# Two rings shared between the sync engine and GpSimd in half tiles every 8 and 12 groups, and the exponentials of layer 0 read from PSUM

## The reference, cut to what matters

```python
edge_index = jnp.stack([src, dst])
h = jnp.maximum(_layernorm(x, axis=-1), 0.0)
x = x + _L0_gnn_ref(edge_index, h, Wq, Wk, Wv, gamma, beta, 8)
h = jnp.maximum(_layernorm(x, axis=-1), 0.0)
x = x + _L1_gnn_ref(h, L1_gnn_beta, edge_index)
...
# layer 0: 8 heads of 16; rows, cols are the two ends of an edge
att = jnp.einsum('ehd,ehd->eh', qE, kE)          # q of one end, k of the other
expAtt = jnp.exp(jnp.clip(att, -10.0, 10.0))
# sums per node of expAtt and of expAtt * vE, then the quotient
...
# layer 1: one head
alpha = jnp.sum(x[row] * x[col], axis=1) / (norm[row] * norm[col]) * beta[0]
# softmax of alpha per node (with its maximum), then sums of alpha * x[col]
```

## Time and profile before

| what | us |
|---|---|
| median of 3 runs | 7085.51 (7075.83 to 7103.98) |
| the profiled execution, own time | 7131.92 |
| its span | 7130.1 |
| layer 0, first to last exponential | about 734 to 3926 |
| layer 1, first to last logit | about 4080 to 7070 |

### The profile page before, as it was taken

How to read it: one execution, slowest core, us unless ns; L and a number is a source line. 1 busy time by engine, 2 the same in 40 slices (tenths; PEclk the granted TensorE clock), 3 DMA queues, 4 the chain that set the end, 5 groups by cost and what they waited for, 6 DMA issues and landing times. The chain is left out here.

```text
span 7130.1 us, 118004 instructions
## 1 busy us (share of the span) xinstructions
PE 4342.2 (61%) x22945; PEld 3749.1 (53%) x22946; DVE 4103.2 (58%) x12176; ACT 2444.7 (34%) x8557; POOL 3380.1 (47%) x3426
## 2 busy tenths in 40 slices
PE   6997555555555555555455156677667676666665
PEld 3886344434443444434344156676666676666665
DVE  8998555555555555555556545555555555555555
ACT  4997111111110111111011544454454444444443
POOL 1334555545454554545454245555555555555552
PEclk8998666666666666666666576666676666776666
DMA  1001222222222222222222112121221121112111
GB/s 35 25 23 34 81 80 76 77 75 77 74 79 77 77 77 75 77 75 79 77 76 73 38 43 48 46 48 47 48 47 47 47 49 46 47 47 49 46 45 39
DMA packets 211652, 414.52 MB, mean 58 GB/s; under 512 B 69399, under 2 KB 103640, under 8 KB 211068
## 3 DMA queue, kind: packets, MB, share of 16 engines
q0 software_dynamic: 135184, 326.41, 17.4%
q1 hardware_dynamic: 74048, 79.04, 3.8%
q10 hardware_dynamic: 1836, 4.03, 0.2%
HBM read 363.52 MB, written 42.48 MB: 57 GB/s over the span
## 5 line engine op out<-in xcount | busy, mean ns | idle before, releaser
L892 POOL DMA_INDIRECT kv_rows<-kv_table,idx_ring x1643 | 1624.6, 989 | 1590.9 <-issue 1003.7
L892 POOL DMA_INDIRECT h_rows<-h_table,idx_ring x1652 | 1566.7, 948 | 1592.7 <-issue 1029.9
L1132 PE MATMUL psum<-vx,hot 128*128 128x136 f32 x3336 | 864.0, 411 | 1135.6 <-DVE acc L1165 1041.0
L1132 PEld LDWEIGHTS psum<-vx,hot 128*128 128x128 f32 x3336 | 696.2, 287 | 1280.3 <-DVE acc L1165 1140.8
L1628 DVE SCALAR_TENSOR_TENSOR h_sb<-h_sb,corr,psum 128x129 f32 x1668 | 582.8, 349 | 931.8 <-PE psum L1586 496.4
L1165 DVE TENSOR_TENSOR acc<-acc,psum 128x136 f32 x1668 | 489.4, 293 | 1006.2 <-remote 850.0
L1576 PE MATMUL psum<-ident,hotl 128*128 128x128 f32 x1668 | 393.9, 381 | 952.7 <-DVE highs L1654 880.6
L1080 ACT ACTIVATE vx<-clip 128x32 f32<-128x32 f32 x417 | 95.2, 229 | 2332.1 <-DVE clip L1209 1878.7
L1576 PEld LDWEIGHTS psum<-ident,hotl 128*128 128x128 f32 x1668 | 258.5, 192 | 1030.6 <-issue 895.4
L1121 PE MATMUL psum<-q_sb,hotT 128*128 x3336 | 712.0, 380 | 32.9 <-issue 23.0
L1121 PEld LDWEIGHTS psum<-q_sb,hotT 128*128 128x128 f32 x3336 | 607.5, 273 | 184.7 <-issue 184.7
(11 more groups left out here) (225 smaller groups left out, 5834.1 us busy)
## 6 DMA issues: line engine op xcount, KB each, us to landing
hand<-kv_table SPq DMA_DIRECT2D x3200, 1.0 KB
hand<-h_table SPq DMA_DIRECT2D x2048, 0.5 KB
own_rows<-own SPq DMA_DIRECT2D x104, 256.0 KB
own<-own_rows SPq DMA_DIRECT2D x104, 256.0 KB
h_rows<-h_table,idx_ring POOLq DMA_INDIRECT x1652
kv_rows<-kv_table,idx_ring POOLq DMA_INDIRECT x1643
kv_table<-kv SPq DMA_DIRECT2D x21, 256.0 KB, 2.1
out<-q_sb SPq DMA_DIRECT2D x2, 1536.0 KB
```

What stands on the lines that cost most here:

```text
L892: pool.indirect_dma_start(out=G[:, k, j, :], out_offset=None, in_=table, in_offset=bass.IndirectOffsetOnAxis(ap=idx[:, k, j:j + 1], axis=0 ...
L1132: last = nc.tensor.matmul(S_ps[j // HALF][:, j % HALF, :], hot[:, k, j * P:(j + 1) * P], vx[:, k, j, :], start=True, stop=True)
```

## The change

1. **Halves.** The tile that SP and POOL share is now cut at row 64 (FROM0 = FROM1 = 64): POOL gathers rows 0 to 63 of it, SP loads rows 64 to 127, and ACT copies those 64. In layer 0 this is tile 3 of every group 8t + 7 (51 times) in place of a whole tile every 16 groups (25 times); in layer 1 every group 12t + 11 (33 times) in place of every 24 groups (16 times). In layer 0 SP still loads 8 rows in each group's step, in layer 1 six in a step.
2. **Loops.** SP, DVE, ACT and POOL now walk with periods of 8 groups (layer 0) and 12 groups (layer 1). The copy by ACT stands at step 5 (layer 0) and step 10 (layer 1).
3. **Exponentials.** In layer 0 ACT takes each exponential twice: into PSUM (`ex_ps`) and into `vx`. The product with the values reads the one in PSUM. DVE waits for one exponential more ahead of it. The PSUM bank comes from the spread node numbers, which have one buffer in place of two: PE's spread of a group waits for DVE's `hotT` of the group before.
4. **Names.** Eight in place of four DMAs write the numbers of the shared tiles to DRAM, and those of layer 0 are read back from there.

```diff
-HAND0 = 16
-BYHAND = P // HAND0
-COPY0_AT = 12
+FROM0, FROM1 = 64, 64
+BYHAND0 = (P - FROM0) // RING0
+COPY0_AT = 5
+BYHAND1, HAND1_AT, COPY1_AT = 6, 10, 10
+TURNS0, TURNS1 = (GROUPS - RING0) // RING0, (GROUPS - RING1) // RING1
...
+def shared(u, t, ring):
+    return u == ring - 1 and not (isinstance(t, int) and t == 0)
...
-        for j in range(GT - hand):
-            pool.indirect_dma_start(out=G[:, k, j, :], out_offset=None, in_=table,
-                                    in_offset=bass.IndirectOffsetOnAxis(ap=idx[:, k, j:j + 1], axis=0)
-                                    ).then_inc(s_gat[k], 16)
-    walk(pool, step, period or ring, first=0, drain=0)
+        for j in range(GT):
+            n = whole if j == GT - 1 and shared(u, t, ring) else P
+            pool.indirect_dma_start(out=G[0:n, u, j, :], out_offset=None, in_=table,
+                                    in_offset=bass.IndirectOffsetOnAxis(ap=idx[0:n, u, j:j + 1], axis=0)
+                                    ).then_inc(s_gat[u], 16)
+    walk(pool, step, ring, first=0, drain=0)
...
-        B_ps = [PS[:, 512 * k:512 * k + GE] for k in (4, 5)]
+        B_ps = PS[:, 2048:2048 + GE]
+        ex_ps = PS[:, 2560:2560 + NEAR * GT * HEADS].rearrange("p (k j h) -> p k j h", k=NEAR, j=GT)
...
-            sp.wait_ge(s_ids, 16 * (per + 4))
+            sp.wait_ge(s_names, 16 * (P // ROW))
+            sp.dma_start(ids.rearrange("o (n c) -> o n c", c=P - FROM0),
+                         names_of(dram, RING0)[:, :, FROM0:P]).then_inc(s_names, 16)
+            sp.wait_ge(s_names, 16 * (P // ROW) + 16)
...
-                for r in range(BYHAND):
-                    p = BYHAND * u + r
+                for r in range(BYHAND0):
+                    p = FROM0 + BYHAND0 * u + r
...
-            walk(sp, step, HAND0, first=0, drain=0, peel=2)
+            walk(sp, step, RING0, first=0, drain=0, peel=2)
...
-                    nc.scalar.activation(vx[:, v, :, D:AW0], clip[:, v, :].rearrange("p (j h) -> p j h", h=HEADS),
-                                         ACT.Exp).then_inc(s_ex, 1)
+                    logits = clip[:, v, :].rearrange("p (j h) -> p j h", h=HEADS)
+                    nc.scalar.activation(ex_ps[:, v, :, :], logits, ACT.Exp)
+                    nc.scalar.activation(vx[:, v, :, D:AW0], logits, ACT.Exp).then_inc(s_ex, 1)
+                    indices(i + RING0, u)
+                    if u == COPY0_AT and shared(RING0 - 1, t, RING0) and (not isinstance(t, int) or t <= TURNS0):
+                        for k in range(2):
+                            act.wait_ge(s_hand[k], 16 * (P - FROM0) // 2 * t)
+                        act.wait_ge(s_vx, RING0 * t)
+                        nc.scalar.copy(G[FROM0:P, RING0 - 1, GT - 1, :], hand[FROM0:P, :]).then_inc(s_copied, 1)
...
-                    need(pe, s_hotT, i + 4)
-                    spread_row(pe, nc, RING0, (u + 5) % RING0, t + (u + 5) // RING0, B_ps[(u + 5) % 2],
+                    need(pe, s_hotT, i + 5)
+                    spread_row(pe, nc, RING0, (u + 5) % RING0, t + (u + 5) // RING0, B_ps,
...
-                    dve.wait_ge(s_ex, i - 1)
+                    dve.wait_ge(s_ex, min(i, GROUPS) if isinstance(i, int) else i)
...
-                                            v[:, :, D:AW0].unsqueeze(3).broadcast_to((P, GT, HEADS, HD)),
+                                            ex_ps[:, k, :, :].unsqueeze(3).broadcast_to((P, GT, HEADS, HD)),
...
-            walk(dve, step, HAND0, first=-4, drain=4)
+            walk(dve, step, RING0, first=-4, drain=4)
...
-                n, b = (t, u - HAND1_AT) if u >= HAND1_AT else (t - 1, u + HAND1 - HAND1_AT)
+                n, b = (t, u - HAND1_AT) if u >= HAND1_AT else (t - 1, u + RING1 - HAND1_AT)
...
-                if u == COPY1_AT and by_hand(HAND1 - 1, t, HAND1) and inside(i):
-                    act.wait_ge(s_hand[0], 16 * HAND_EVEN1 * t)
-                    act.wait_ge(s_hand[1], 16 * (P - HAND_EVEN1) * t)
-                    act.wait_ge(s_sum, HAND1 * t + HAND1 - RING1)
-                    nc.scalar.copy(G[:, RING1 - 1, GT - 1, :], hand[:, :]).then_inc(s_copied, 1)
+                if inside(i) and u == COPY1_AT and shared(RING1 - 1, t, RING1) and (not isinstance(t, int) or t <= TURNS1):
+                    act.wait_ge(s_hand[0], 16 * EVEN1 * t)
+                    act.wait_ge(s_hand[1], 16 * (P - FROM1 - EVEN1) * t)
+                    act.wait_ge(s_sum, RING1 * t)
+                    nc.scalar.copy(G[FROM1:P, RING1 - 1, GT - 1, :], hand[FROM1:P, :]).then_inc(s_copied, 1)
...
-            walk(dve, step, HAND1, first=0, drain=9)
+            walk(dve, step, RING1, first=0, drain=9)
```

More of the change, by code:

```diff
@@ L74 @@
 QUADS = -(-GROUPS // FOUR)
-HAND0 = 16
-BYHAND = P // HAND0
-COPY0_AT = 12
[L78 to L83, removed]
+FROM0, FROM1 = 64, 64
+BYHAND0 = (P - FROM0) // RING0
+COPY0_AT = 5
+BYHAND1, HAND1_AT, COPY1_AT = 6, 10, 10
+BATCHES1 = -(-(P - FROM1) // BYHAND1)
+EVEN1 = sum(min(BYHAND1, P - FROM1 - BYHAND1 * b) for b in range(0, BATCHES1, 2))
+TURNS0, TURNS1 = (GROUPS - RING0) // RING0, (GROUPS - RING1) // RING1
 PART = 7
@@ L865, in last_words, with gather_groups @@
     return dram["sorted"][WHOLE * P * P:WORDS].rearrange("(q c) -> q c", c=P)
[L868 to L881, removed]
+def shared(u, t, ring):
+    return u == ring - 1 and not (isinstance(t, int) and t == 0)
+def gather_groups(pool, ring, table, G, idx, s_idx, s_read, s_gat, s_go, whole):
     def step(i, u, t):
@@ L890, in step, with names_of @@
         pool.sem_inc(s_go, 1)
-        for j in range(GT - hand):
-            pool.indirect_dma_start(out=G[:, k, j, :], out_offset=None, in_=table,
-                                    in_offset=bass.IndirectOffsetOnAxis(ap=idx[:, k, j:j + 1], axis=0)
-                                    ).then_inc(s_gat[k], 16)
-    walk(pool, step, period or ring, first=0, drain=0)
+        for j in range(GT):
[4 more added lines that the diff above has]
+    walk(pool, step, ring, first=0, drain=0)
+def names_of(dram, ring):
+    turn = ring * GT // ROW
+    first = (2 * ring * GT - 1) // ROW
+    turns = (GROUPS - ring) // ring
+    rows = dram["names"].rearrange("k a c -> (k a) c")
+    return rows[first:first + turn * (turns - 1) + 1:turn, :].rearrange("(o n) c -> o n c", o=1)
 def own_quad(dram, q, n):
@@ L1012, in hand_rows @@
             def hand_rows(u, t):
-                if isinstance(t, int) and not 1 <= t < GROUPS // HAND0:
+                if isinstance(t, int) and not 1 <= t <= TURNS0:
                     return
@@ L1018, in hand_rows @@
                     _, named[0] = nc.values_load_multi_w_load_instructions(
-                        ids[0:1, ds(P * t + BYHAND * u, 2 * BYHAND)], engines=[sp.engine], min_val=0, max_val=NPAD - 1,
-                        skip_runtime_bounds_check_because="the numbers that the gathers use")
-                for r in range(BYHAND):
-                    p = BYHAND * u + r
-                    sp.dma_start(hand[p:p + 1, :], dram["kv"][ds(named[0][BYHAND * (u % 2) + r], 1), :]
+                        ids[0:1, ds((P - FROM0) * t - (P - FROM0) + BYHAND0 * u, 2 * BYHAND0)], engines=[sp.engine],
+                        min_val=0, max_val=NPAD - 1, skip_runtime_bounds_check_because="the numbers that the gathers use")
+                for r in range(BYHAND0):
+                    p = FROM0 + BYHAND0 * u + r
+                    sp.dma_start(hand[p:p + 1, :], dram["kv"][ds(named[0][BYHAND0 * (u % 2) + r], 1), :]
                                  ).then_inc(s_hand[u % 2], 16)
@@ L1079, in step @@
                     need(act, s_sum, i + 1 - NEAR)
-                    nc.scalar.activation(vx[:, v, :, D:AW0], clip[:, v, :].rearrange("p (j h) -> p j h", h=HEADS),
-                                         ACT.Exp).then_inc(s_ex, 1)
-                    indices(i + RING0, u % RING0)
-                    keep_own(i + NEAR, (u + NEAR) % RING0, 2 * t + (u + NEAR) // RING0)
-                if u == COPY0_AT and by_hand(HAND0 - 1, t, HAND0) and inside(i):
-                    for k in range(2):
-                        act.wait_ge(s_hand[k], 16 * P // 2 * t)
-                    act.wait_ge(s_vx, HAND0 * t + HAND0 - RING0)
-                    nc.scalar.copy(G[:, RING0 - 1, GT - 1, :], hand[:, :]).then_inc(s_copied, 1)
+                    logits = clip[:, v, :].rearrange("p (j h) -> p j h", h=HEADS)
[7 more added lines that the diff above has]
+                        nc.scalar.copy(G[FROM0:P, RING0 - 1, GT - 1, :], hand[FROM0:P, :]).then_inc(s_copied, 1)
+                    keep_own(i + NEAR, (u + NEAR) % RING0, t + (u + NEAR) // RING0)
             for g in range(NEAR):
                 keep_own(g, g, 0)
-            walk(act, step, HAND0, first=0, drain=0)
+            walk(act, step, RING0, first=0, drain=0)
         @block.tensor
@@ L1544, in _ @@
                 widen_own(g, g, 0)
-            walk(act, step, HAND1, first=0, drain=7)
+            walk(act, step, RING1, first=0, drain=7)
         @block.tensor
```

84 lines of the change are left out of this document (38 added, 46 removed).

## The result

The changed kernel takes 7224.98 us (median of four runs, 7216.26 to 7247.29), the kernel before 7094.74 (7075.83 to 7130.73). The ratio is 1.0182, with a 95% interval from 1.0133 to 1.0231: slower by some 130 us. The forecast was 7190, in a range from 6990 to 7300.

A forecast was written before the change was run, and what follows sets the result against it. Layer 0 was taken to go at SP's pace against POOL's bursts, with DVE held between. Terms 94 + 20 - 12 - 22 + 27 = +107 on 7131.92, less 46.4 to the median, gave 7190 us, range 6990 to 7300.

The forecast's parts named there:

- The bound: Layer 0: SP's row loading against POOL's unbroken gather bursts sets the pace, 124.0 us a turn of 16 groups, DVE held between.
- The pace behind SP: Layer 0: POOL's bursts of twelve gathers, with DVE held until they end, take 22.9 us for three groups.
- The half turn: Layer 0, 8 groups from copy to copy: 64.0 us against 62.05, +1.95 in each of 48, +94 us.
- The handshake: Layer 0, from SP's last row issued to the end of ACT's copy: 1.8 us, now in each 8 groups.
- The short branch: Layer 0 loops of SP and DVE: halved, a branch takes 0.3 us in place of 2.4 and 2.9.
- The joining: Layer 0 after each copy: POOL's short burst and the next join into twelve unbroken gathers, from +2.9 us.
- The rival that rested on its absence: No joining, layer 0: bursts stay as before, half turn 60.7 us, whole 7027 us; chance 0.26.
- The first turn: Layer 0's first turn ends at group 15, not 31; group 31 comes later: +20 us.
- The half gather: POOL's gather of 64 rows in layer 0 takes between half and a whole one's time: -12 us, ends 0 and -25.
- The exponentials from PSUM: Layer 0: gathers begun inside DVE's `vx` no longer lengthened: -22 us, ends 0 and -29.
- Layer 1: DVE's branches in layer 1 stay dear and there are 17 more: +27 us, ends 0 and +49.

The follow-up runs named there:

- p3: The changed kernel with 32 instead of 64 rows of each shared tile loaded in layer 0: 6807.80 us, ratio 0.9761 to the kernel before.
- p1: The kernel before, with a pause (POOL sets a 128x256 scratch tile) behind each group's gathers in both layers: 6306.16 us, ratio 0.9044.
- e4: The changed kernel with layer 0's loops written out for 16 groups, tile still shared in halves every 8: 7240.37 us, ratio 1.0213 to the kernel before.
- e2: The changed kernel without exponentials in PSUM, spread numbers again with two banks: 7213.84 us, ratio 1.0180 to the kernel before.
- e3: The changed kernel with layer 1's loops written out for 24 groups, tile still shared in halves every 12: 7177.67 us, ratio 1.0134 to the kernel before.
- c4: The changed kernel with POOL's 128x256 memset behind each group's gathers and layer 1's loops written out for 24 groups: 6768.32 us, ratio 0.9562 to the kernel before.
- after: The changed kernel itself, against the kernel before: 7224.98 us, ratio 1.0182.
- p4: The changed kernel with POOL's 128x256 memset behind each group's gathers in both layers: 6490.39 us, ratio 0.9308 to the kernel before.

## Why the prediction was right, step by step

**The bound.** Right. SP's rows set layer 0's pace (`p3`: with half of the rows gone the ratio falls from 1.018 to 0.976), and POOL's bursts slow SP and hold DVE (`p1`). The pace behind SP was mis-sized: 7.0 us a group, not 22.9/3.

A rival not named so far is that SP is slow because it waits for ACT and PE before it stores and loads the node numbers. The trace of the kernel before excludes it: between 950 and 3300 us the view of SP's waits has one line, 0.3 us for ACT. It is SP's instructions that are slow. The view of line 1023, from 2086 to 2098 inside the burst of the earlier trace rows and then from 2101 to 2104 behind it, shows five rows in 12 us and eight in 3. Inside, the address of a row takes 0.72 us at the median, behind it 0.04 (minimum, median and maximum in ns):

```profile
SPq L1031 <- ACT own L1066: 0.3, 1, 0.3
...
L1023 SPq FUSED_REGOPS  x5: 5/717/1402, 2085.8 to 2094.5; - x5
L1023 SPq DMA_DIRECT2D hand<-kv_table x5: 17/687/724, 2087.3 to 2096.7; - x5
...
L1023 SPq DMA_DIRECT2D hand<-kv_table x8: 227/228/228, 2100.9 to 2103.7; - x8
L1023 SPq FUSED_REGOPS  x7: 37/37/37, 2101.1 to 2103.6; - x7
```

What a "remote" wait is, the same trace tells: PE's last product for the sum of the earlier trace rows has ended at 2090.1 by its record, and its semaphore `s_sum` is raised only at 2100.3, which is also when SP's instructions are quick again. DVE's semaphore for the third `vx` of that burst is raised at once, at 2091.9. Why PE's is held back and DVE's is not stays open.

**The half turn, +1.95 us, +94 in all.** Right in sign, mis-sized, and for the wrong main reason. Measured: 63.12 against 62.38, +0.74, and groups 31 to 415 took 2974.9 us before, 3013.0 after, +38, where the forecast's terms had 94 - 12 - 22 = +60. The rows until the second cycle's end (47) and the last stretch from row to copy (1.7 us) came out near. The first cycle took 20.4 us and not 22.9, and the last 17 rows 15.6 us where 13.6 was forecast; the two errors nearly cancel. Set side by side the rows take as long as before. The handshake was in the sum, but not as the loss: SP loads nothing for 3.15 us in every half turn. The short branch shortens the wait for the first row, from 2.66 to 1.43 us, and doubling the copies costs more. This division is read from the traces; no run took the handshake alone away while SP was the pace.

**The joining.** It happens in each of the 48 half turns. In `e4` it makes the rows 2.1 us longer, where 64.1 - 60.7 = 3.4 was forecast. In the changed kernel its price can't be read, as no half turn is without it, but with the shorter first cycle the rows take 59.97 us, no more than before. The rival that rested on its absence had its price wrong too: half turns without it took 63.8 us, 1.2 of them SP's dear branch, where 60.7 was worked out for a cheap one.

**The first turn, +20.** Group 31 came 212.9 us after the first clip before and 227.1 after, +14.

**The half gather, -12.** Near zero, its upper end. The 51 half gathers take 0.90 us each at the median, where whole ones take 0.95: 2 us in all. The mean gather of layer 0 is the same, and POOL issues 25 more:

```profile
L892 POOL DMA_INDIRECT kv_rows<-kv_table,idx_ring x1643 | 1624.6, 989 | 1590.9 <-issue 1003.7
```

```profile
L881 POOL DMA_INDIRECT kv_rows<-kv_table,idx_ring x1668 | 1649.0, 989 | 1625.4 <-DVE vx L1186 1158.7
```

**The exponentials from PSUM, -22.** Zero, also an end (`e2`). Gathers begun inside `vx` are no longer long, none of 99 against 59 of 62 in the kernel before; but those begun inside `hot`, with both operands in SBUF too, are now 198 and were 153. The lengthening in sum is 72 us and was 70. Many of the collisions moved to the next operation. The nearer comparison is `e2`, whose loops are those of the changed kernel: there 150 gathers begun inside `vx` and 157 inside `hot` are lengthened, and all gathers of layer 0 together take 1665.2 us, against 1649.0 in the changed kernel. So the exponentials in PSUM do take 16 us of gathers off POOL, and in layer 0's time nothing of it is seen.

```profile
L881 POOL DMA_INDIRECT kv_rows<-kv_table,idx_ring x1668 | 1665.2, 998 | 1599.1 <-DVE vx L1184 1133.6
```

**Layer 1, +27.** The branches stay dear as forecast, but the size was wrong: +65 in the profile, 68 by the ratios. The branch takes DVE 3.42 us and not 2.9, so that its 31 taken branches take 106.0 us where 14 took 41.5. How much of these 64.5 us reaches layer 1's time is known only roughly, 34 us by `e3`. Counted at nothing were the halves, likely some 30 us by `c4` and `e3`. Why they would cost there was not tried; 16 more gathers at 1.25 us each would be 20.

The sum, +107 against +115 in the profile and +130 between the medians, is nearer than its terms: two that came out at zero and not negative, and a dearer layer 1, made up for a half turn that was forecast too long.

## What to carry to other kernels

Where two engines share a job through a handshake, split the time from one handshake to the next into work and the time in which the slower one has none; halving the job halves only the first. A DMA by index took POOL 0.90 us for 64 rows and 0.95 for 128, so sharing one in halves gives it next to nothing back. And when waits end with another engine's row of work and not with their own producer, break that row: 1.1 to 1.2 us between each four gathers and the next, in place of 0.3, were worth 9.6%.

## What the runs showed of the hardware

Unbroken gathers on POOL slow what is not on POOL. In the kernel before SP issues 0.50 rows a us during the unbroken rows of twelve (both ends taken 2 us later, as the effect lags) and 1.81 a us between them; over a turn that makes 1.06, and 1.28 with the pause. DVE stands up to 9.3 us for PE's sums (1500 to 3500 us), as PE's semaphore is raised some 10 us after the product's recorded end (2090.1 and 2100.3 us).

How long the break has to be is known in steps only, from a gather's end to the next one's start: 1.12 us after four gathers gives 6.0 us a group in layer 0, 0.97 gives 6.15 and a whole that is 149 us longer, 0.49 after eight gives nothing.

A loop's branch on the same code took DVE 3.42 us at the median in one build and 3.00 in another (`after` and `e4`, layer 1). The kernel before differs by 1.6% between two of the chips. Layer 0 of the changed kernel with the pause differs by 6% between `p4` and `c4`, which are two builds on two chips; which of the two does it was not tried. So only runs on one chip should be set side by side, and single layers even there with care.
